# S4D convolution and gathered low-rank layer on one core: TensorE's heads in loops of six, three slots instead of four, and K's first set stored in two halves

## The reference, cut to what matters

```python
def _L0_cond_ref(u, log_dt, C, log_A_real, A_imag, D, length):   # u: (128, 32, 512)
    dt = jnp.exp(log_dt); A = -jnp.exp(log_A_real) + 1j * A_imag  # (32, 64)
    dtA = A * dt[:, None]
    Ct = (C[..., 0] + 1j * C[..., 1]) * (jnp.exp(dtA) - 1.0) / A
    K = 2.0 * jnp.einsum('hn,hnl->hl', Ct, jnp.exp(dtA[:, :, None] * jnp.arange(512))).real
    y = irfft(rfft(u, 1024) * rfft(K, 1024)[None], 1024)[..., :512]   # causal convolution
    y = y + u * D[:, None]
    return y * (jnp.arange(512)[None, :] < length[:, None])[:, None, :]

def _L1_cond_ref(x, adapter_ids, base_weight, base_bias, lora_A_w, lora_B_w):
    result = jnp.einsum('bsd,od->bso', x, base_weight) + base_bias
    A, Bw = lora_A_w[adapter_ids], lora_B_w[adapter_ids]          # 128 of 32 adapters, rank 16
    return result + jnp.einsum('bsr,bor->bso', jnp.einsum('bsd,brd->bsr', x, A), Bw)

x = x + _L0_cond_ref(x, log_dt, C, log_A_real, A_imag, D, itok_B_78_3631)
x = x + _L1_cond_ref(x, itok_B_6_15, base_weight, base_bias, lora_A_w, lora_B_w)
```

## Time and profile before

| | |
|---|---|
| three runs | 210.38 us median (210.12 to 210.66) |
| the profiled execution | 210.57 us |
| its span | 208.5 us |
| TensorE products, loads of weights | 91 %, 80 % of the span |
| VectorE, ScalarE, POOL | 81 %, 58 %, 43 % |
| chain that ended last | PE 87 %, DMA 6 %, DVE 4 % |
| DMA in the whole span | 271 GB/s |

### The profile page before, as it was taken

How to read it: one execution, slowest core, us unless ns; L and a number is a source line. 1 busy time by engine, 2 the same in 40 slices (tenths; PEclk the granted TensorE clock), 3 DMA queues, 4 the chain that set the end, 5 groups by cost and what they waited for, 6 DMA issues and landing times.

```text
span 208.5 us, 4394 instructions
## 1 busy us (share of the span) xinstructions
PE 190.8 (91%) x1063; PEld 166.4 (80%) x1063; DVE 168.1 (81%) x368; ACT 120.9 (58%) x354; POOL 90.3 (43%) x144
## 2 busy tenths in 40 slices
PE   0049999999999999899999999999999999999994
PEld 0037999999999899787888888888888888888883
DVE  3985598789799976877999978788888878888662
ACT  2798974343736446237767656657566565656530
POOL 4850000001356778085564645546455464545500
PEclk9999999999999999999999999999999999999999
DMA  5973999999999999983767666677776676765324
GB/s 141 400 310 105 377 410 409 409 413 406 412 411 407 409 407 422 339 262 105 257 238 247 217 207 228 214 201 224 213 222 204 216 229 201 218 200 186 103 101 151
DMA packets 21520, 56.46 MB, mean 271 GB/s; under 512 B 3266, under 2 KB 3970, under 8 KB 21250
## 3 DMA queue, kind: packets, MB, share of 16 engines
q1 hardware_dynamic: 18002, 47.55, 62.2%
q0 software_dynamic: 2560, 8.39, 13.3%
q10 hardware_dynamic: 944, 0.36, 0.7%
...
## 4 chain that ended last, share of the span: by engine, by line
PE 87%; DMA 6%; DVE 4%; POOL 1%; issue 1%; DVEq 0%
PE z_ps L932 26%; PE y_ps L971 20%; PE k_ps L971 20%; PE z_ps L959 7%; DMA strip<-k_pad 5%; PE y_ps L904 3%; PE y_ps L998 2%; PE y_ps L997 2%; PE k_ps L998 2%; PE k_ps L997 2%; PE k_ps L913 1%; DMA par<-params 1%; PE y_ps L1020 1%; PE k_ps L1020 1%; PE y_ps L981 1%
## 5 line engine op out<-in xcount | busy, mean ns | idle before, releaser
L932 PE MATMUL z_ps<-xp,strip 128*128 128x512 f32 (+3 forms) x384 | 63.4, 326 | 0.3 <-DMA strip<-k_pad 0.3
L932 PEld LDWEIGHTS z_ps<-xp,strip 128*128 128x128 f32 x384 | 59.3, 196 | 4.3 <-DMA strip<-k_pad 0.4
L417 POOL DMA_INDIRECT b_hl<-b_tab,b_idx x32 | 37.7, 1178 | 15.3 <-issue 8.5
L412 POOL CAST ag<-a_hl 128x128 fp32r x64 | 23.3, 367 | 41.0 <-PE z_ps L959 30.4
L971 PE MATMUL y_ps<-w_hi,xp 128*128 128x512 f32 x120 | 39.5, 390 | 0.0
L971 PE MATMUL k_ps<-w_hi,xp 128*128 128x512 f32 x120 | 39.5, 390 | 0.0
L550 ACT ACTIVATE ag<-a_hl 128x64 fp32r x128 | 25.6, 249 | 20.5 <-issue 20.3
L462 ACT ACTIVATE xp<-z_all 128x512 fp32r<-128x512 f32 x32 | 19.7, 627 | 19.7 <-PE z_ps L932 18.2
L741 DVE TENSOR_TENSOR xp<-z_all,xp 128x512 fp32r<-128x512 f32 x32 | 26.5, 827 | 5.3 <-ACT xp L462 5.2
L971 PEld LDWEIGHTS y_ps<-w_hi,xp 128*128 128x128 f32 x120 | 22.5, 188 | 4.3
L971 PEld LDWEIGHTS k_ps<-w_hi,xp 128*128 128x128 f32 x120 | 22.5, 188 | 4.2
...
## 6 DMA issues: line engine op xcount, KB each, us to landing
...
w_sb<-w_t SPq DMA_DIRECT2D x2, 512.0 KB, 10.0
...
```

The source lines that it names most:

```text
L412: last = g.tensor_copy(ag[:, s, :, :, q, :].rearrange("p c e r -> p e c r"), src)
L417: g.indirect_dma_start(out=b_hl[:, t % BS, :].bitcast(F32), out_offset=None, in_=b_tab, in_offset=bass.IndirectOffsetOnAxis(ap=b_idx[:, t: ...
L932: last = nc.tensor.matmul(z_ps[:, h % ZS, m * P:L], strip[:, h % SS, m * P:(m + 1) * P, t], xp[:, h % XS, 0:LC - m, e, :], start=(n == 0), ...
```

## The change

- K comes in five groups, two of four heads for the first set (GROUPS, SETS), and three of eight. The first two are stored by SP, each as its remainder is done, with pair 7 of x between the stores; the third also by SP, ahead of strip 6. ScalarE stores only the last two. All of the first three are multiplied before head 0, and the two late ones stand behind the heads 7 and 13.
- The strips of head 0 and head 1 come in two halves each.
- k_hi goes: ScalarE rounds straight into k_sb (rounded_rows). In the late groups VectorE adds D to lag 0 (k_first_lag) instead of a product of TensorE.
- xp has three slots in use for the convolution and z_ps three banks (CS, x_slot, z_bank). TensorE's heads 2 to 31 are five rounds of a loop body of six heads, the first two rounds with a late group behind them. In the body, head h waits for h-1 masked heads.
- TensorE's padding begins as soon as POOL has filled its operand: 12, 5, 4, 4 and 5 products, then K's two half groups, then 10, 3 and 5 more, then the third group.
- POOL's and ScalarE's early work: the sign and the factor 2 of the coefficients are applied by two small ScalarE operations (the table holds 2 and -2), one addition of POOL and one multiplication by 0.5 go, two operations on mm move up. iota of the mask and eye wait for the third group's factors.
- Two loads of SP move a head later (24 to 25, 26 to 27).
- At the first tiles: x tile 2 is loaded ahead of the tables' stores and tile 3 ahead of the bias; h_down goes ahead of the rounding of tile 2, h_masked ahead of its remainder, h_remainder ahead of tile 3.

```diff
-GROUPS = ((0, 8), (8, 16), (16, 24), (24, 32))
+SETS = ((0, 8), (8, 16), (16, 24), (24, 32))
...
 G = 8
 NG = len(GROUPS)
+BY_SP = 3
...
 SS = 6
 ZS = 4
+CS = 3
 KS = 2
 XP = 2
...
 PRE = 8
-X_AT = {7: 8, 10: 9, 13: 10, 15: 11, 18: 12, 20: 13, 22: 14, 24: 15}
+X_AT = {7: 8, 10: 9, 13: 10, 15: 11, 18: 12, 20: 13, 22: 14, 25: 15}
 IDS_AT = 5
-A_AT, B_AT, W_AT = {9: 0, 12: 1}, {17: 0, 19: 1}, {24: 0, 26: 1}
+A_AT, B_AT, W_AT = {9: 0, 12: 1}, {17: 0, 19: 1}, {24: 0, 27: 1}
 XT_AT = 30
 SPLIT_A = {17: 0, 18: 1, 19: 2, 20: 3}
 SPLIT_B = {23: 0, 24: 1, 25: 2, 26: 3}
 SPLIT_W = {29: 0, 30: 1, 31: 2}
-K_AFTER = {2: 7, 3: 14}
-WARM_0, WARM_1 = 15, 2
+K_AFTER = {3: 7, 4: 13}
+K_SLOT = (0, 1, 0, 1, 1)
+WARM = (12, 5, 4, 4, 5)
+WARM_K = (10, 3, 5)
 MAGS_AT = {4: (24, 28), 5: (28, 32)}
 STEPS_AT = {2: (4, 5, 6, 7, 8, 9), 3: (10, 11, 12, 13, 14, 15)}
...
+        def x_slot(h):
+            return (h + 1) % CS + 1
+        def z_bank(h):
+            return h % CS + 1
...
+        def store_k(engine, k):
+            (h0, h1), s = GROUPS[k], K_SLOT[k]
+            engine.dma_start(k_pad[h0:h1, P:PAD, :].rearrange("h (a c) e -> a h (c e)", a=NA),
+                             k_sb[:, s, 0:h1 - h0, :, :].rearrange("a h c e -> a h (c e)").bitcast(F32)
+                             ).then_inc(k_stored[s], 16)
...
-            for n in range(2, PRE):
+            for n in range(2, PRE - 1):
                 load_pair(n)
+            for k in range(KS):
+                sp.wait_ge(k_lo_done, k + 1)
+                store_k(sp, k)
+                if k == 0:
+                    load_pair(PRE - 1)
...
             for h in range(NH):
                 for k, (h0, h1) in enumerate(GROUPS):
                     if h == h0:
-                        sp.wait_ge(k_stored, 16 * (k + 1))
+                        sp.wait_ge(k_stored[K_SLOT[k]], 16 * turn_of(k))
+                if h == SS:
+                    sp.wait_ge(k_lo_done, BY_SP)
+                    store_k(sp, BY_SP - 1)
                 if h >= SS:
                     sp.wait_ge(conv_done, h + 1 - SS)
-                if h == 0:
-                    load_strip(h, 0, 0, L // 2, strip_begun)
-                    load_strip(h, 0, L // 2, L, strip_landed[0])
+                if h < 2:
+                    load_strip(h, h, 0, L // 2, strip_begun[h])
+                    load_strip(h, h, L // 2, L, strip_landed[h])
                 else:
...
             load_x_tile(1, 1)
+            load_x_tile(2, 2)
             store_table(0, b_hl[:, :, :].bitcast(F32), tab_hi_stored)
             store_table(1, b_lo, tab_lo_stored)
+            load_x_tile(3, 3)
             sp.dma_start(bias_sb[:, :], bias.to_broadcast((P, L))).then_inc(bias_in, 16)
-            load_x_tile(2, 2)
-            load_x_tile(3, 3)
...
+            pool.wait_ge(zeroed, 1)
+            g.memset(xp[:, 0, :, 0, :].bitcast(F32), 1.0).then_inc(warm_ready, 1)
+            pool.wait_ge(warm_ready, 1)
...
-            link(g.tensor_scalar(par[:, 3:5, :], par[:, 3:5, :], tab[:, NL:NL + 1], None, ALU.mult))
...
-            link(g.tensor_tensor(sm[:, 2, :], sm[:, 0, :], sm[:, 1, :], ALU.add))
-            link(g.tensor_scalar(rc[:, 0, :], sm[:, 2, :], 0.5, None, ALU.mult))
+            link(g.tensor_tensor(rc[:, 0, :], sm[:, 0, :], sm[:, 1, :], ALU.add))
+            pool.wait_ge(signed, 2)
+            link(g.tensor_tensor(sm[:, 6:8, :], par[:, 4:6, :], twice(ai), ALU.mult))
...
+            link(g.tensor_tensor(mm[:, 1, 1, :], sm[:, 6, :], sm[:, 4, :], ALU.subtract))
+            link(g.tensor_tensor(mm[:, 1, 0, :], sm[:, 5, :], sm[:, 7, :], ALU.add))
...
-            link(g.tensor_tensor(mm[:, 1, 1, :], sm[:, 6, :], sm[:, 4, :], ALU.subtract))
-            link(g.tensor_tensor(mm[:, 1, 0, :], sm[:, 5, :], sm[:, 7, :], ALU.add))
...
-            pool.wait_ge(factors, 2)
+            pool.wait_ge(factors, 2 * (KS + 1))
...
+                if h >= CS:
+                    act.wait_ge(conv_done, h + 1 - CS)
+                act.activation(xp[:, x_slot(h), :, 0, :], z_all[:, h, :, :], ACT.Copy).then_inc(xc_hi_done, 1)
...
+            def rounded_rows(k):
+                n, s = GROUPS[k][1] - GROUPS[k][0], K_SLOT[k]
+                act.wait_ge(k_done, k + 1)
+                if k in K_AFTER:
+                    act.wait_ge(d_added, 1 + list(K_AFTER).index(k))
+                if k >= KS:
+                    act.wait_ge(k_stored[s], 16 * turn_of(before(k)))
+                act.activation(k_sb[:, s, 0:n, :, 0], k_ps[0:NA, s, 0:n * NC].rearrange("a (h c) -> a h c", c=NC),
+                               ACT.Copy).then_inc(k_hi_done, 1)
...
+                rounded_rows(k)
...
+            act.wait_ge(table_in, 16)
+            act.activation(par[:, 3:5, :], par[:, 3:5, :], ACT.Copy, scale=tab[:, NL:NL + 1]).then_inc(signed, 1)
+            act.activation(par[:, 2:6:3, :], par[:, 2:6:3, :], ACT.Copy, scale=2.0).then_inc(signed, 1)
...
-            group_sines(1)
+            magnitudes(8, 10)
+            rounded_rows(0)
+            magnitudes(10, 12)
+            rounded_rows(1)
+            magnitudes(12, 16)
+            set_sines(1)
             split_x(1)
-            magnitudes(16, 18)
-            group_store(1)
+            magnitudes(16, 17)
+            rounded_rows(2)
+            magnitudes(17, 19)
             split_x(2)
-            magnitudes(18, 24)
-            split_x(3)
...
+            h_down(0, 0)
             x1_hi(2, 2, True)
-            h_down(0, 0)
...
+            def k_first_lag(k):
+                (h0, h1), s = GROUPS[k], K_SLOT[k]
+                dve.wait_ge(k_done, k + 1)
+                lag_0 = k_ps[0:1, s, 0:(h1 - h0) * NC:NC]
+                V.tensor_tensor(lag_0, lag_0, d_sb[:, h0:h1], ALU.add).then_inc(d_added, 1)
...
-            multiply()
-            scale()
-            turns, phases, whole, fraction, multiply, scale = group(1)
+            for k in range(KS):
...
+            turns, phases, whole, fraction = set_of(1)
+            k_low(0)
...
+            k_low(1)
...
-            k_low(0)
...
+            multiply, scale = group(KS)
...
-            k_low(1)
+            k_low(KS)
             masks()
             remainder(2)
-            remainder(3)
-            beside = {h: do for k, at in STEPS_AT.items() for h, do in zip(at, group(k))}
-            for h in range(XS, NH):
-                head(h - XS)
+            beside = {h: do for k, at in STEPS_AT.items() for h, do in zip(at, set_of(k) + group(k + 1))}
+            for h in range(CS, NH):
+                head(h - CS)
                 for k, last in K_AFTER.items():
-                    if h == last + XS:
+                    if h == last + CS:
+                        k_first_lag(k)
                         k_low(k)
                 remainder(h)
...
             x1_of(2, 2, 0)
+            h_masked(0, 0)
             x1_remainder(2, 2)
-            h_masked(0, 0)
+            h_remainder(0, 0)
             x1_of(3, 3, 0)
-            h_remainder(0, 0)
...
                 pe.wait_ge(factors, 2 * (k + 1))
                 if k >= KS:
-                    pe.wait_ge(k_lo_done, k + 1 - KS)
-                for i in range(h1 - h0):
...
+                    pe.wait_ge(k_lo_done, before(k) + 1)
+                group(k, K_SLOT[k], h1 - h0)
+            def late_group(lap):
+                k0, k1 = K_AFTER
+                pe.wait_ge(factors, lap * 2 + 2 * (k0 + 1))
+                pe.wait_ge(k_lo_done, lap * (before(k1) - before(k0)) + before(k0) + 1)
...
+            def first_head(h):
+                pe.wait_ge(strip_begun[h], 16)
+                pe.wait_ge(xc_lo_done, h + 1)
+                products(h)
+            def six_heads(lap):
+                for s in range(2, SS + 2):
+                    pe.wait_ge(strip_landed[s % SS], 16 * (lap + (s // SS + 1)))
+                    pe.wait_ge(xc_lo_done, lap * SS + (s + 1))
+                    pe.wait_ge(z_masked, lap * SS + (s - 1))
+                    products(s)
+            pe.wait_ge(warm_ready, 1)
+            keep_warm(WARM[0])
+            for n, (ready, count) in enumerate(((turn_ready, 1), (angle_ready, 1), (cs_ready, 1), (sines_ready, 1))):
+                pe.wait_ge(ready, count)
+                keep_warm(WARM[1 + n])
             pe.wait_ge(d_in, 16)
             pe.wait_ge(zeroed, 2)
-            group(0)
-            pe.wait_ge(xc_hi_done, 1)
-            keep_warm(WARM_0)
-            group(1)
-            keep_warm(WARM_1)
-            for h in range(NH):
-                head(h)
-                for k, last in K_AFTER.items():
-                    if h == last:
-                        group(k)
+            early_group(0)
+            early_group(1)
+            keep_warm(WARM_K[0])
+            pe.wait_ge(reduced, 2)
+            keep_warm(WARM_K[1])
+            pe.wait_ge(sines_ready, 2)
+            keep_warm(WARM_K[2])
+            early_group(KS)
+            first_head(0)
+            first_head(1)
+            with pe.Fori(0, len(K_AFTER)) as lap:
```

(4 more changed lines are left out.)

149 lines of the change are left out of this document (72 added, 77 removed).

## The result

The changed kernel took 212.26 us as the median of four runs (212.12 to 212.77); the kernel before, on the same chip, 210.27 (210.12 to 210.66). The ratio is 1.0094, with a 95% interval from 1.0082 to 1.0106: slower by 2.0 us, where 0.7 was forecast. The span of the profiled execution is 210.4 us against 208.5.

What follows compares the result with a forecast made beforehand. TensorE was taken to bound the convolution, transfers and VectorE close behind. Gains of 1.85, 0.26, 0.4 and 0.3 against waits of 0.8, 0.4, 1.2 and 1.1 gave +0.7 us: 211.1 us from 210.38, range 209.2 to 212.5.

Steps and rivals of the forecast that it cites:

- Slower: Whole kernel: time up by over 0.3% (0.63 us); chance 0.45, against same 0.35 and faster 0.2.
- The front: Before the convolution: earlier factors, store and strips let head 0 start at 19.5 instead of 21.35 us, -1.85 us.
- Four waits for VectorE: Convolution: TensorE waits at the group behind head 7 (+0.8), head 10 (+0.4), group behind head 13 (+1.2), head 20 (+1.1).
- Head 10: Convolution: VectorE is held in K's low part, so mask 8 ends at 40.8 with TensorE ready at 40.5; +0.4 us.
- The stepping of VectorE's list: Convolution: VectorE's list stepped at present pitches puts the late groups' factors at 35.9 and 49.8 us.
- Nothing for heads 0 and 1: First heads: strips come 1.7 us earlier, issue to landing as now, and moving pair 7 costs nothing; 0 us.
- The group's product: Two late K groups: one extra product goes from each, 0.13 us twice, -0.26 us.
- a loop costs nothing: TensorE's convolution loops: register work and branches charged at nothing, as unrolled and looped tiles both take 3.67 us.
- Strip 25: Late convolution: the strip goes ahead of the x pair and the waits give the queue time; -0.4 us (0 to -0.45).
- The seam: First tiles: h_down goes ahead of tile 2's split, removing TensorE's 0.27 us wait for ACT's gather; -0.3 us.
- A: Rival, convolution: VectorE keeps up, waits below 2.2 us together, ends faster, 208.3 to 209.7 us; chance 0.2.
- D: Rival, convolution loops: 0.05 us per looped head adds 1.5, waits absorb 0.5, giving 212.1 us; chance 0.12.

Runs made afterwards that it cites:

- e9: Changed kernel with TensorE's list written out and head h waiting for the mask of head h-3 instead of h-2: 210.94 us, ratio 1.0007 to the kernel before.
- e7: Changed kernel with four slots of split inputs, four banks, the mask wait on head h-4 and TensorE's list written out: 209.88 us, ratio 0.9954 to the kernel before.
- e4: Changed kernel with VectorE's six steps of each late set one head earlier: 211.50 us, ratio 1.0044 to the kernel before.
- e2: Changed kernel with the load of x pair 7 behind strip 4 instead of between K's two stores: 211.42 us, ratio 1.0041 to the kernel before.
- e11: Changed kernel, list written out, mask of head h-3, steps and w splits one head earlier, pair 7 behind strip 4: 210.20 us, ratio 0.9984 to the kernel before.
- e8: e7 with the load of x pair 7 moved behind strip 4: 210.35 us, ratio 0.9955 to the kernel before.
- e3: Changed kernel with TensorE's heads 2 to 31 and late groups written out, no loop, same waits: 212.25 us, ratio 1.0102 to the kernel before.

## Why the prediction was right, and where it was off

Slower was forecast as the likeliest sign, and the time lies inside the range, at its upper side: 1.2 us above the forecast.

- *The front, -1.85.* Right: head 0 at 19.34 for 19.5. The steps are in the trace as forecast: factors at 12.45, the first store on SP at 13.91, the padding products at 0.24 to 0.27 each once under way (18 in 4.69), sine of the second set at 16.48, factors at 18.56.
- *Four waits for VectorE, 3.5 together.* Right in place and size: 0.97, 1.26 for the second and third, 1.10, so 3.33 by the starts, and 2.9 as named idle time (0.80, 0.2, 0.98, 0.92). Head 10 came smaller than its 0.4. The stepping of VectorE's list with 0.6 us pitches put the factors at 35.9 and 49.8 where they came at 36.59 and 50.51; head 2's late start is in that. That the strict mask wait is the whole of head 20's stop is shown by e9; that slots, banks and strict wait together are the cause of all of them by e7, which does not part them; that about half of the group waits is only the place of the steps by e4.
- *Nothing for heads 0 and 1.* This step failed: +0.72. The text said that the strips would be 1.7 us earlier with the landing "as now", and took the move of pair 7 for free, "when SP waits anyway". SP's time was free; the queue behind it was not. The first half took 3.9 us instead of 3.0, and the third strip set the start of head 2. With the pair out of the way head 2 starts 0.34 to 0.68 us earlier (e2, e11, e8); what holds back the rest is open.
- *The group's product, -0.26.* The product was worth its 0.13 (0.57 in e3 for 0.70), but the loop's end took it back where a group precedes it. The claim that a loop costs nothing was read from tiles, where TensorE's queue holds work; behind eight short products it costs 0.16 to 0.19. By the profiles little of these 0.35 us was on the path of the time, since VectorE's waits stood behind them (e3).
- *Strip 25, -0.4.* It came: no head behind 20 waits for a strip. But it hung on TensorE's own lateness, as the forecast partly said: with the stop at head 20 gone, head 26 waits again, 0.32 us in e9 and 0.24 in e7. And the same stretch gave it back at the first tile, whose wait grew from 0.78 to 1.33. The forecast had no term for this: with three slots ScalarE's last split waits for head 28 instead of head 27, so what follows on ScalarE and POOL, the splits of w, moves 3.6 us later (one head, and 1.6 by which the heads themselves are later) and meets VectorE's additions. That this meeting makes the wait is read from the rows of several profiles, not from a run that moved POOL alone.
- *The seam, -0.3.* Right: -0.35, with the gap ahead of tile 1's products gone.
- *The rivals.* A would have needed waits of under 2.2 us; it was 3.33. D's slower heads don't exist (e3).
- *The whole.* The terms that failed, 0.72 at the first heads, 0.35 at the groups and 0.47 between head 20 and the first tile, all made the kernel slower; the front, the waits and the seam came out better by 0.16, 0.17 and 0.05. That the time stayed inside the range is owed to the range, not to the sum.
